# Front stage of a graph network kernel: degrees as a row of the counted adjacency; input transposes and four right products between the groups of the one-hot loop; angles and bias on GpSimd

## The reference, cut to what matters

```python
h = relu(layernorm(x))
# layer 0: mean over incoming edges, plus the node itself
deg = segment_sum(1, dst);  agg = segment_sum(h[src], dst) / max(deg, 1)
x = x + relu(agg @ W_l + b_l + h @ W_r)
# layer 1 (transformer, 4 blocks): a condition per node from the noise level
ph = noise * freqs                                  # 625 x 32
emb = concat([sin(ph), cos(ph)])
cond = silu(emb @ f_w1 + f_b1) @ f_w2 + f_b2
# attention over edges: needs, for each pair (src, dst), the number of edges between them
# layer 2 (GCN): edge_weight = sigmoid(edge_attr_3 @ conf_w.T + conf_b), degrees by src
# layer 3 (edge network): 20000 edges, two dense layers with mish
```

## Time and profile before

| | us |
|---|---|
| median of 3 runs | 1644.84 (1644.69, 1644.84, 1652.89) |
| span of the profiled execution | 1645.6 |
| busy PE, PE weight loads | 1558.5 (95%), 1222.4 (74%) |
| busy DVE, ACT, POOL | 1187.6 (72%), 1100.3 (67%), 679.0 (41%) |
| the one-hot loop on PE | 16.4 to 102.7 |
| `front` after the loop, to its last "left" product | 102.7 to 171.7 |
| first matmul of the transformer | 179.4 |

### The profile page before, as it was taken

One profiled execution on the slowest core, in us unless ns is written; L12 is line 12 of the kernel. 1 busy time (PEld: TensorE's weight loads), 2 busy tenths in 40 slices (PEclk: granted clock), 3 DMA queues, 4 the chain that ended last, 5 costly groups with the idle time before them and its releaser, 6 DMA issues. The chain is left out here.

```text
span 1645.6 us, 24993 instructions
## 1 busy us (share of the span) xinstructions
PE 1558.5 (95%) x8530; PEld 1222.4 (74%) x8530; DVE 1187.6 (72%) x1898; ACT 1100.3 (67%) x1534; POOL 679.0 (41%) x498
## 2 busy tenths in 40 slices
PE   5789899999999999999999999999999999999987
PEld 5765687878788778877854777777777777777874
DVE  8978646555565646465623599888998898899877
ACT  9841545544564546454530699999999999999963
POOL 3410200120012001200302788788888888888601
PEclk9999899999999999999999999999999999999989
DMA  3001320022012200202007867677777777777710
GB/s 106 0 20 66 94 80 26 26 60 82 26 33 84 77 1 33 84 32 91 27 1 232 160 140 151 144 145 149 147 149 146 149 148 143 149 148 149 172 40 32
DMA packets 107046, 153.94 MB, mean 94 GB/s; under 512 B 42042, under 2 KB 47034, under 8 KB 106466
## 3 DMA queue, kind: packets, MB, share of 16 engines
q0 software_dynamic: 72832, 87.84, 27.6%
q1 hardware_dynamic: 34146, 65.21, 12.5%
HBM read 141.02 MB, written 11.73 MB: 93 GB/s over the span
## 5 line engine op out<-in xcount | busy, mean ns | idle before, releaser
L1787 POOL DMA_INDIRECT edge_gathered<-dst_table,edge_index x158 | 268.5, 1699 | 59.5 <-issue 54.0
L223 PE MATMUL edge_z2p<-edge_w_hi,edge_h_hi 128*128 128x512 f32 x628 | 256.7, 409 | 1.7 <-DVE edge_late L2110 0.9
L223 PE MATMUL edge_z2p<-edge_w_hi,edge_h_lo 128*128 128x512 f32 x628 | 248.6, 396 | 0.0
L223 PE MATMUL edge_z2p<-edge_w_lo,edge_h_hi 128*128 128x512 f32 x628 | 248.3, 395 | 0.0
L1756 POOL DMA_INDIRECT edge_gathered<-src_table,edge_index x158 | 201.7, 1276 | 85.4 <-POOL edge_index L1750 30.6
L977 POOL TENSOR_TENSOR h<-h,tr_row_b 128x512 f32<-128x512 f32 x40 | 59.2, 1514 | 271.6 <-ACT C L1222 271.3
L966 POOL TENSOR_TENSOR tr_cw<-w_c,tr_cw 32x1024 fp32r<-32x1024 f32 x7 | 16.6, 2373 | 350.2 <-ACT tr_cw L1182 350.2
L223 PEld LDWEIGHTS edge_z2p<-edge_w_hi,edge_h_hi 128*128 128x128 f32 x628 | 117.9, 188 | 54.9 <-issue 29.8
L223 PEld LDWEIGHTS edge_z2p<-edge_w_hi,edge_h_lo 128*128 128x128 f32 x628 | 118.1, 188 | 28.7
L223 PEld LDWEIGHTS edge_z2p<-edge_w_lo,edge_h_hi 128*128 128x128 f32 x628 | 118.1, 188 | 24.7
L2110 DVE TENSOR_TENSOR edge_late<-edge_z2p,w_c 128x1024 f32<-128x1024 f32 x79 | 96.7, 1224 | 44.1 <-PE edge_z2p L223 43.5
(11 more groups left out here) (366 smaller groups left out, 4022.7 us busy)
## 6 DMA issues: line engine op xcount, KB each, us to landing
w_c<-in_attr_T SPq DMA_DIRECT2D x78, 128.0 KB
agg<-edge_sum_rows POOLq DMA_DIRECT2D x36, 128.0 KB
w_a<-in_wv SPq DMA_DIRECT2D x4, 1024.0 KB, 5.3
w_b<-in_wq SPq DMA_DIRECT2D x4, 1024.0 KB, 5.5
w_a<-in_wk SPq DMA_DIRECT2D x4, 1024.0 KB, 7.7
w_b<-in_wo SPq DMA_DIRECT2D x4, 1024.0 KB, 6.9
w_a<-in_m SPq DMA_DIRECT2D x4, 1024.0 KB, 5.5
w_b<-in_m SPq DMA_DIRECT2D x4, 1024.0 KB, 5.2
```

What stands on the lines that cost most here:

```text
L223: mm = pe.matmul(out, a, b, start=(n == 0), stop=(n == last))
L1787: pool.indirect_dma_start(out=from_rows[ring][:, j, :].bitcast(F32), out_offset=None, in_=k.dst_table, in_offset=bass.IndirectOffsetOnAxis ...
```

## The change

- **Degrees.** The last column of `from_onehot` (node 639, which is padding) is set to 1 once by POOL, and the compares cover COMPARED = 628 columns, so row 639 of the counts becomes the sum over all sources, the degree of each destination. "degT" reads that row straight out of `sums` (with a column of the identity that picks partition 127). The products "deg" (10 matmuls), the two copies and the tile `deg` go. The GCN products use 114 rows of the last tile, so that the row stays out of them.
- **PE.** PLAIN = 4 rounds stay a loop, five rounds (groups 16 to 35) are written out: behind each of groups 16 to 20 come the four transposes of one tile of h, behind each of groups 20 to 35 one of the four matmuls of a "right" product, so four of the five "right" products are made there. One round follows as a loop. These products use the two PSUM banks outside `ps` in turn ("beside"); the six banks of `ps` serve "agg" and "left". After the loop PE makes the fifth "right", the hidden layer, five aggregates, the condition, "degT", three aggregates, "left".
- **POOL.** Its first 32 groups are written out; behind every second group from 4 to 26 it makes one of 12 steps of the angles (nine with one input, three additions of two tiles, because the fused multiply-add becomes two instructions). After its loop it adds b_l to the five right parts.
- **ACT** takes the transposes and the right products (without the bias) inside the loop, then the fifth one after it; it takes the aggregates, and sums the counts with `accum_out`.
- **DVE** loses the angles, the taking of "right" and "agg", the sum of the counts, and the two "deg" copies; its other steps after the loop come in a new order.
- **SP** loads `cond_w` into `w_c` when the last "right" product is made.

The diff, cut to its core:

```diff
-    PEELED = 5
+    PEELED = 9
+    PLAIN = 4
+    ANGLED = 8
+    SLOTS = 4
+    COMPARED = -(-NODES // 4) * 4
...
-                    {"one": [p[:, j * D:(j + 1) * D] for p in ps for j in range(3)] + [t[:, :] for t in single]})
+                    {"beside": [t[:, :] for t in single], "one": [p[:, j * D:(j + 1) * D] for p in ps for j in range(3)]})
+        INSIDE = (PEELED - PLAIN) * RING - SLOTS
+        RIGHT = INSIDE // KF
+        AGG = [(m, f) for m in range(KF) for f in range(2)]
+        AHEAD = 5
         for i in range(NT):
-            plan.add(("hT", i), "sca")
+            plan.add(("hT", i), "sca", "beside")
         for i in range(NT):
-            plan.add(("right", i), "vec")
+            plan.add(("right", i), "sca", "beside")
         for f in range(2):
-            plan.add(("hidden", f), "vec")
...
+            plan.add(("hidden", f), "vec", "beside")
+        for m, f in AGG[:AHEAD]:
+            plan.add(("agg", m, f), "sca")
         for f in range(2):
-            plan.add(("deg", f), "vec")
...
+            plan.add(("cond", f), "vec", "beside")
+        plan.add(("degT", 0), "vec", "beside")
+        for m, f in AGG[AHEAD:]:
+            plan.add(("agg", m, f), "sca")
...
             @block.gpsimd
+                for a in range(RING):
+                    pool.memset(from_onehot[a][:, :, COMPARED:NP - 1], 0.0).then_inc(consts_made, 1)
+                    pool.memset(from_onehot[a][:, :, NP - 1:NP], 1.0).then_inc(consts_made, 1)
...
+                for u in range(ANGLED * RING):
+                    weigh(u, u % RING)
+                    if u == RING:
+                        pool.wait_ge(loaded_cond, 16 * 6)
+                    if u >= RING and u % 2 == 0:
+                        angle(u // 2 - RING // 2)
+                with pool.Fori(0, n * (GROUPS // RING) + (GROUPS // RING - ANGLED)) as t:
                     for a in range(RING):
...
+                        weigh(t * RING + (ANGLED * RING + a), a)
+                pool.wait_ge(loaded_w, 16 * 3)
+                for i in range(NT):
+                    plan.need(pool, ("right", i))
+                    pool.tensor_tensor(own_part[:, i, :], own_part[:, i, :], bl[:, :], ALU.add).then_inc(bias_added, 1)
...
             @block.scalar
+                beside.update({PLAIN * RING + SLOTS + i: lambda i=i: take_turned(i) for i in range(NT)})
+                INSIDE_LOOP = [i for i in range(RIGHT) if PLAIN * RING + SLOTS + (i + 1) * KF + 3 < PEELED * RING]
+                beside.update({PLAIN * RING + SLOTS + (i + 1) * KF + 3: lambda i=i: take_right(i) for i in INSIDE_LOOP})
...
+                for i in range(len(INSIDE_LOOP), RIGHT):
+                    take_right(i)
+                act.wait_ge(angle_step, ANGLE_STEPS)
                 act.activation(emb[:, :], ph[:, :], ACT.Sin).then_inc(emb_ready, 1)
                 act.preload_act_table_set(LOG_AND_EXP)
+                act.wait_ge(added, n * SPANS + (SPANS + 2))
                 for i in range(NT):
                     act.wait_ge(maxed, i + 1)
                     act.activation(k.logc[:, i, :], k.logc[:, i, :], ACT.Ln).then_inc(logs_ready, 1)
+                    if i == 1:
+                        for j in range(RIGHT, NT):
+                            take_right(j)
                 act.wait_ge(cz_ready, 2)
                 act.activation(ce[:, :], cz[:, :], ACT.Exp, scale=-1.0).then_inc(ce_ready, 1)
+                take_agg(*AGG[0])
...
+                for i in range(2):
+                    sum_counts(i)
+                for i in range(2, NT):
+                    act.wait_ge(has_ready, i - 1)
+                    sum_counts(i)
+                    take_agg(*AGG[i - 1])
+                for i in range(NT):
+                    scale_W(i)
+                    if i + NT - 1 < len(AGG):
+                        take_agg(*AGG[i + NT - 1])
...
             @block.tensor
+                with pe.Fori(0, PLAIN) as t:
                     for a in range(RING):
...
+                        sum_group(t * RING + a, a, t * (RING // SHARE) + a // SHARE)
+                for u in range(PLAIN * RING, PEELED * RING):
+                    sum_group(u, u % RING, u // SHARE)
+                    i, slot = u - PLAIN * RING, u - PLAIN * RING - SLOTS
+                    if i < NT:
+                        bank = plan.open(pe, ("hT", i))
+                        pe.wait_ge(h_ready, i + 1)
+                        plan.made(turn(pe, bank, h[:, i, :], k.ident[:, :]))
+                    if slot == 0:
+                        pe.wait_ge(loaded_w, 16 * 3)
+                    if 0 <= slot < RIGHT * KF:
+                        right_chunk(slot // KF, slot % KF)
+                with pe.Fori(0, n * (GROUPS // RING) + (GROUPS // RING - PEELED)) as t:
+                    for a in range(RING):
+                        sum_group(t * RING + (PEELED * RING + a), a, t * (RING // SHARE) + (PEELED * RING + a) // SHARE)
...
                 bank = plan.open(pe, ("degT", 0))
-                plan.need(pe, ("deg", 1))
+                last_rows = slice(P - PART, P)
                 for i in range(NT):
-                    mm = pe.matmul(bank[:, i:i + 1], deg[0:1, i * P:(i + 1) * P], k.ones[0:1, 0:1], start=True, stop=True)
+                    mm = pe.matmul(bank[:, i:i + 1], sums[last_rows, NT - 1, 0, i * P:(i + 1) * P],
+                                   k.ident[last_rows, P - 1:P], start=True, stop=True)
                 plan.made(mm)
+                for m, f in AGG[AHEAD:]:
+                    aggregate(m, f)
...
             @block.vector
-                        ins = dve.tensor_scalar(from_onehot[a][:, j, :], iota16[:, 0:NP],
+                        ins = dve.tensor_scalar(from_onehot[a][:, j, 0:COMPARED], iota16[:, 0:COMPARED],
...
                 for i in range(NT):
                     dve.tensor_scalar(k.logc[:, i, :], sums[:, i, 0, 0:NP], 1.0, None, ALU.max).then_inc(maxed, 1)
-                    bank = plan.take(dve, ("right", i))
-                    plan.took(("right", i), dve.tensor_tensor(own_part[:, i, :], bank, bl[:, :], ALU.add))
-                step(dve.tensor_reduce(k.has[:, :], sums[:, :, 0, 0:NP], AX.X, ALU.add))
...
-                take_agg(0, 0)
+                for i in range(3):
+                    sum_W(i)
                 dve.wait_ge(ce_ready, 1)
                 step(dve.tensor_scalar(ce[:, :], ce[:, :], 1.0, None, ALU.add))
                 step(dve.reciprocal(ce[:, :], ce[:, :]))
                 dve.tensor_tensor(cz[:, :], cz[:, :], ce[:, :], ALU.mult).then_inc(silu_ready, 1)
...
+                for i in range(3, NT):
+                    sum_W(i)
+                dve.wait_ge(has_ready, NT)
+                dve.tensor_scalar(k.dis[:, :], k.has[:, :], 1.0, None, ALU.max).then_inc(maxed, 1)
+                dve.wait_ge(maxed, NT + 1)
+                step(dve.tensor_scalar(k.has[:, :], k.has[:, :], 1.0, None, ALU.min))
+                for i in range(NT):
+                    no_edge(i)
                 for f in range(2):
                     bank = plan.take(dve, ("cond", f))
...
+                    dve.wait_ge(bias_added, i + 1)
```

More of the change, by code:

```diff
@@ L261, in front @@
         shift = sb("shift", [P, NT])
-        deg = sb("deg", [1, NP])
-        noise, ph, turns = sb("noise", [EMB, NP]), sb("ph", [EMB, NP]), sb("turns", [EMB, NP])
+        noise, ph, turns, reduced = (sb(n, [EMB, NP]) for n in ("noise", "ph", "turns", "reduced"))
         emb = sb("emb", [EMB, NP])
@@ L421, in _ @@
                         last_tile(u, a)
-                for i in range(NT):
-                    bank = plan.take(act, ("hT", i))
-                    plan.took(("hT", i), act.activation(hT[:, :, i * P:(i + 1) * P], cols(bank, P), ACT.Copy))
-                act.wait_ge(angle_ready, 1)
+                for i in range(len(INSIDE_LOOP), RIGHT):
+                    take_right(i)
+                act.wait_ge(angle_step, ANGLE_STEPS)
                 act.activation(emb[:, :], ph[:, :], ACT.Sin).then_inc(emb_ready, 1)
                 act.preload_act_table_set(LOG_AND_EXP)
+                act.wait_ge(added, n * SPANS + (SPANS + 2))
                 for i in range(NT):
@@ L438, in _ @@
                 act.activation(k.dis[:, :], k.dis[:, :], ACT.Exp, scale=-0.5).then_inc(logs_ready, 1)
-                for i in range(NT):
-                    act.wait_ge(W_joined, i + 1)
-                    act.activation(sums[:, i, 1, 0:NP], sums[:, i, 1, 0:NP], ACT.Copy, scale=1.0 / SCALE_HI).then_inc(W_summed, 1)
                 def first_norm(i):
@@ L478, in _ @@
                 pe.sem_inc(added, 2)
+                pe.wait_ge(consts_made, PADS)
                 n = sweeps(pe)
[L480 to L495 removed]
@@ L497, in _, with sum_group @@
-                pe.wait_ge(added, n * SPANS + (SPANS + 2))
-                for i in range(NT):
-                    bank = plan.open(pe, ("hT", i))
-                    pe.wait_ge(h_ready, i + 1)
-                    plan.made(turn(pe, bank, h[:, i, :], k.ident[:, :]))
```

(33 more changed lines are left out.)

150 lines of the change are left out of this document (78 added, 72 removed).

## The result

| | before | changed | |
|---|---|---|---|
| median, us | 1645.96 (20 runs) | 1650.04 (20 runs) | ratio 1.0023, 95% interval 1.0017 to 1.0029 |
| span of the profiled execution | 1645.6 | 1647.7 | |
| PE starts pair 20 | 60.21 | 68.80 | |
| PE is through the loop's last pair | 102.66 | 121.26 | |
| PE starts "left" | 154.24 | 156.34 | |

I had forecast 1644 us and no change; the kernel is slower by 0.17 to 0.29%, some 4 us. That is under the half per cent that I took as the limit of a measurement, but with twenty runs it is clear. So the traces differ by 2.1 us and the medians by 4.1.

What follows compares the result with a forecast made beforehand. DVE was taken to bound the loop and PE the stretch behind it; +8.1 + 6.7 + 3.2 - 18.7 - 0.1 = -0.8 us from 1644.84 gave 1644 us, range 1639 to 1650, 8 in 10 within 1632 to 1653.

Steps and rivals of the forecast that it cites:

- The mechanism in the loop: In the loop: DVE sets the pace, and whatever POOL does while DVE has compares left is added to DVE's half.
- An instruction each: In the loop: DVE and POOL take turns by single instructions, so a compare of 0.37 us beside POOL takes about 1.2.
- Rival 1: In the loop: DVE does not lose to the angles and the bias, its half stays 4.34 us; 1633 us, chance 0.17.
- Part 1: Angle steps on POOL in the loop: one-input 0.7 us, two-input 1.6, added to DVE's halves 4 to 20; +8.1 us.
- Part 2: PE's added transposes and "right" matmuls in the loop: PE becomes the bound from pair 20; +6.7 us.
- Part 3: Loop's end: POOL's additions of b_l take turns with DVE's last compares, so PE waits; +3.2 us, bounds 0 to 4.5.
- Part 4: After the loop: "left" starts 32.9 us behind the end of PE's last pair in place of 51.6; -18.7 us.
- the wait at "degT": After the loop: PE waits 2.7 us ahead of "degT" for DVE's taking of "cond"; bounds 0 to 5.
- loss of clock in pairs 4 to 18: In the loop: PE, with less to do there, might be granted less than full clock; named as a way to be wrong, unpriced.
- the small terms: Loop and ahead of it: 12 fewer compare columns -0.2 us, eight small memsets and a semaphore +0.1; -0.1 us in the sum.
- Rival 2: In the loop: angle steps cost 2.0 us each, like the slow two-input additions; 1657 us, slower, chance 0.09.
- Rival 3: After the loop: waits are longer, since ACT is late and DVE comes late to "cond"; 1648 us, chance 0.12.

Runs made afterwards that it cites:

- e1: The changed kernel without POOL's angle steps but for the last clamp, made of the raw noise level (condition not the reference's): 1639.78 us.
- e2: The changed kernel with a second operation that does nothing (add 0.0) in each one-operation angle step: 1645.70 us.
- e3: The changed kernel with POOL's five additions of the bias held back until the sixth aggregate is made: 1646.24 us.
- e4: The changed kernel with the degree column made behind the last three aggregates instead of ahead of them: 1642.24 us.
- e5: The changed kernel with degree column behind the last aggregates, bias after the sixth aggregate, and one-operation angle steps written as multiply then add: 1634.47 us.
- e6: The changed kernel with all five "right" products behind the loop again, the transposes staying inside: 1656.26 us.
- e7: The kernel before with the degree row alone (ones in the last column, compares of 628 columns, no product with ones): 1641.14 us.

## Why the prediction was wrong, point by point

- **The mechanism in the loop: right in the main.** DVE and POOL take turns, and POOL's steps lengthen DVE's halves though nobody waits for them. e1 shows it. "An instruction each" did not hold for the long steps. Rival 1 (DVE does not lose) fell with it: it gave 1633 and needed pair 20 at 60; it was at 68.80.
- **Part 1, +8.1 us: right in sum by luck, wrong in its terms.** Pair 20 starts 8.6 us later. I priced a one-input step at 0.7; the six steps with one operation in the halves 4 to 20 took 1.84 to 2.05, nearly three times that; all nine steps together 15.8 us, which by my rule would have been 7.7 more than foretold. Two things stood against it. A long step lets a compare in on the way: DVE's additions, one to a half, start at 32.99, 38.54, 44.05, 49.33, 54.83, 60.53 and 66.03 in the change, so a half with a step of 1.5 to 2.05 us grew by 1.1 to 1.5 over the 4.21 of e1, and not by the step's length. And the written-out POOL shortened every half by 0.1. The rows from which I took the price, a memset and a select, hold other operations; e2 shows that the price hangs on these. The rule of the Trainium skill that I set beside it (GPSIMD Engine Reference, Engine selection: one input at about line rate) fits the cheap combinations roughly (0.71 to 1.02 us against the estimate of 0.53) and is off by more than three times for the others; the measurement decides.
- **Part 2, +6.7: right.** 49.2 us foretold from pair 20 to the end, without the bias; 121.26 - 68.80 - 3.1 = 49.4 measured. A "right" matmul and its group take 2.54 us and not 2.60, and DVE's long steps give that back between pairs 22 and 26.
- **Part 3, +3.2: right**, 3.1 by e3. The three parts put the end of the loop at 102.66 + 18.0 = 120.7 (the prediction says 120.8 in another place); it is at 121.26.
- **Part 4, -18.7: this step failed.** "left" was to start 32.9 us behind the loop's end; it starts 35.1 behind it, a gain of 16.5. The waits were as foretold: 2.25 (2.7) for the taking of the condition and 0.62 (0.8) for the last aggregate. But I priced the wait at "degT" by its length alone and let the 9.4 us behind it go at full clock. The granted clock fell to 0.50 there, and they took 12.45: +3.0 us. e4 takes the wait away, the clock stays at 1.00 and the same work takes 9.5. I had looked for a loss of clock in pairs 4 to 18 only; there it also came (40 matmuls in 5.12 us behind a wait of 2.35, where 3.47 is usual), and it cost nothing, since DVE was the bound: from the start of pair 4 to that of pair 20 it is 42.2 us in the change and 42.2 in e4, where the clock stayed at 1.00.
  The Trainium skill (TensorE: Matmul & The Clock Gate, Part 1, The HAM clock gate) says that the array's clock is halved when PE has been idle. This trace agrees: the granted clock was 1.00 up to the wait of 2.25 us and 0.50 behind it. That not every wait has this effect is shown by the loops of e3 and e4, with 1.00 behind 2.81 and 2.86 us.
- **The sum.** Foretold were -0.8 us. The loop ended 18.6 later than before and not 18.0, Part 4 was 2.2 short (3.0 for the clock, less 0.9 of waits and roundings that were smaller), and the small terms of -0.1 fall away: 0.6 + 2.2 + 0.1 makes +2.1, which is what the traces show at the start of "left". The measured time lies 6.0 above the forecast of 1644, at the upper end of its range: 2.9 are these misses, 1.1 that the kernel before came to 1645.96 over twenty runs and not to 1644.84, and 2.0 are not located, since the profiled executions lay on different sides of their medians.
- **Rival 2** had the right sign and a part of its cause: steps of 2.0 us occurred, but cost 1.1 to 1.5 each. Rival 3 (longer waits) did not occur.

## What to carry to other kernels

Price a wait of the matmul engine not by its length alone: where it falls behind the last place with slack, the work that follows it may run at half clock (here 2.3 us of waiting cost 5.2), so look in the written order for something else that could stand in that place; three aggregates were there. Work given to GpSimd is not free because GpSimd is idle: while DVE runs instructions that take turns with it, much of its length is added to DVE's (here 0.8 us for a step of 1.0, 1.1 to 1.5 for steps of 1.5 to 2.0), so put it where another engine is the bound, and measure the very combination of operations. When a change has many parts, a single part alone (here the degree row, 5.3 us) can be worth more than the whole.

## What I had not expected of the hardware

- GpSimd's `tensor_scalar` on 64x640 floats took 0.71 to 1.02 us with multiply-add or minimum-maximum, 1.84 to 2.05 with one operation, 2.42 to 2.60 with add-add or subtract-add. Writing a plain addition or subtraction as multiply by 1.0 and add made it 1.8 to 2.5 times as fast (e5).
- A long GpSimd step lets a DVE compare in before its end: in a step of 1.84 us one compare got through.
- PE's clock went from 2.4 to 1.2 GHz behind the wait of 2.25 us ahead of the degree column in all five kernels that have it (the change, e1, e2, e3, e6), and in the loop behind waits of 1.92 (e3), 2.21 (e2), 2.35 and 2.82 (the change), 2.69 and 2.86 us (e6). Yet in the loop it stayed up behind 1.92 (e4), 2.02 (e5), 2.81 and 2.86 us (e3, e4). So the length of a wait does not settle it (1.92 and 2.86 went both ways), and how much of the spread between runs comes from that was not measured.
- With GpSimd's program written out and not in a loop, each of DVE's halves was 0.10 us shorter (4.31 in e7, 4.21 in e1).
